# A two-layer transformer kernel on one core: three pairs of PSUM banks in turn for the first attention, and one bank for the row maxima of the second

## What is computed

```python
xn = _layernorm(x)
x  = x + attn0(xn) + ffn0(xn)          # layer 0
xn = _layernorm(x)
x  = x + attn1(xn) + ffn1(xn)          # layer 1

def attn0(x):      # 16 heads of 64 channels, causal; "dense" below
    k, q, v = W_K x, W_Q x, W_V x
    scores = tril(k . q) ; attn = softmax(scores / sqrt(64))
    z = v . attn ; return W_O z

def ffn0(x):       # conv, 16 heads of 8 channels with rotary angles, causal softmax,
    ...            # projection, then a routed layer of 4 experts; "early", "ahead", "after"
def attn1(x):      # block-wise softmax, 16 heads of 8 channels; "behind"
def ffn1(x):       # 4-bit rounding of inputs and weights, gate, up, down; "behind"
```

## Time and profile before

| | us |
|---|---|
| median of 3 executions | 3603.09 (3598.25 to 3603.40) |
| the profiled execution's own time | 3598.52 |
| its span, first to last instruction | 3596.7 |
| PE busy | 3086.5 (86%) |
| DVE, ACT, POOL busy | 2093.3, 1787.1, 860.3 |
| mean granted TensorE clock, of full speed | 0.937 |

### The profile page before, as it was taken

The page is one execution under the profiler, slowest core; times in us unless marked ns, Lnnn a source line. Parts: engine busy times, 40 slices in busy tenths (PEclk is TensorE's granted clock), DMA queues, the critical chain, the costliest instruction groups (busy, mean ns, idle before and its releaser), DMA issues.

```text
span 3596.7 us, 53224 instructions
## 1 busy us (share of the span) xinstructions
PE 3086.5 (86%) x19535; PEld 1705.8 (47%) x19535; DVE 2093.3 (58%) x4810; ACT 1787.1 (50%) x4252; POOL 860.3 (24%) x1140
## 2 busy tenths in 40 slices
PE   2689898998989899998989889898988989898864
PEld 1245455454545545454545545454554545454432
DVE  5454665756566575657656565665656566554432
ACT  0245555555545455555545555554555555455421
POOL 0000222313222131323123132312213131222323
PEclk7699999999999999999999999999999999999965
DMA  4130303020020302002030301103020110200000
GB/s 104 20 44 1 52 2 47 9 36 20 13 43 2 55 2 44 12 17 40 1 55 2 44 12 22 35 2 55 2 44 12 24 31 7 47 2 14 6 11 3
DMA packets 112901, 89.39 MB, mean 25 GB/s; under 512 B 11203, under 2 KB 107269, under 8 KB 112645
## 3 DMA queue, kind: packets, MB, share of 16 engines
q1 hardware_dynamic: 93956, 70.25, 12.8%
q0 software_dynamic: 4096, 8.40, 0.8%
q10 hardware_dynamic: 14592, 7.34, 0.7%
HBM read 27.05 MB, written 16.19 MB: 12 GB/s over the span
## 4 chain that ended last, share of the span: by engine, by line
PE 59%; DVE 12%; POOL 10%; issue 9%; ACT 5%; DMA 2%; SPq 1%; POOLq 0%; ACTq 0%; DVEq 0%
PE ps L1584 6%; PE ps L1601 6%; PE ps L1819 4%; PE ps L1743 4%; PE ps L1722 4%; PE ps L1656 3%; PE ps L1645 3%; PE ps L1623 3%; DVE nma L1210 3%; PE ps L1632 3%; PE ps L1574 2%; PE ps L1703 2%; PE ps L1884 2%; PE ps L1561 2%; PE ps L1587 2%
## 5 line engine op out<-in xcount | busy, mean ns | idle before, releaser
L877 ACT ACTIVATE share_a<-ps,nma 128x128 f32<-128x128 f32 (+3 forms) x1024 | 530.9, 525 | 443.7 <-DVE nma L1210 442.5
L1210 DVE TENSOR_REDUCE nma<-ps 128x2 f32<-128x256 f32 (+3 forms) x512 | 420.1, 823 | 407.5 <-PE ps L1587 405.4
L945 ACT ACTIVATE share_z<-ps 128x512 f32<-128x512 f32 (+1 forms) x704 | 378.3, 559 | 372.1 <-PE ps L1724 241.7
L1275 DVE TENSOR_REDUCE nmx<-ps 128x1 f32<-128x384 f32 (+3 forms) x704 | 426.1, 635 | 173.9 <-PE ps L1705 162.4
L722 POOL TENSOR_TENSOR vn<-va,rla 128x512 f32<-128x512 f32 x128 | 133.4, 1042 | 1359.1 <-DVE rla L1181 1359.1
L1601 PE MATMUL ps<-share_a,vn 128*64 128x512 f32 (+3 forms) x2048 | 351.4, 492 | 35.7 <-POOL vn L722 34.7
L1703 PE MATMUL ps<-kst,qst 96*128 96x128 bf16 (+3 forms) x1024 | 269.6, 317 | 71.1 <-DMA kst<-part 34.4
L1722 PE MATMUL ps<-qst,kst 99*128 99x512 bf16 (+3 forms) x1024 | 261.6, 304 | 28.2 <-ACT share_z L945 14.9
L798 POOL TENSOR_TENSOR share_s<-share_s 128x352 f32<-128x352 f32 (+1 forms) x80 | 80.1, 1001 | 770.7 <-DVE share_s L1084 770.5
L1601 PEld LDWEIGHTS ps<-share_a,vn 128*64 128x64 f32 x2048 | 150.8, 151 | 227.9 <-issue 154.2
L1584 PE MATMUL ps<-kq_odd 64*128 64x128 f32 (+3 forms) x1024 | 220.5, 508 | 38.7 <-ACT share_a L877 36.9
(11 more groups left out here) (250 smaller groups left out, 5727.0 us busy)
## 6 DMA issues: line engine op xcount, KB each, us to landing
qst<-part SPq DMA_DIRECT2D x144, 128.0 KB
kst<-part SPq DMA_DIRECT2D x144, 128.0 KB
share_r<-h_sorted SPq DMA_DIRECT2D x16, 448.0 KB, 3.5
y_sorted<-share_a ACTq DMA_DIRECT2D x16, 448.0 KB, 3.0
xin<-in_L_attn_x SPq DMA_DIRECT2D x16, 256.0 KB, 3.9
xk<-xn SPq DMA_DIRECT2D x16, 256.0 KB, 17.5
xres<-in_L_attn_x SPq DMA_DIRECT2D x16, 256.0 KB
out<-xn SPq DMA_DIRECT2D x16, 256.0 KB, 17.4
```

The source lines that it names most:

```text
L877: activation(pa[:, h % 4, OFF[t]:OFF[t] + P * (t + 1)], ps[:, b + k, 0:P * (t + 1)], ACT.Exp, bias=nma[:, h, t:t + 1], accum_out=la[:, h, ...
L945: activation(pt[:, n % 2, h % 4:h % 4 + k, 0:wd], src, ACT.Exp, scale=SCALE_B)\
L1210: v.tensor_reduce(nma[:, 2 * p:2 * p + 2, t], ps[:, b:b + 2, 0:P * (t + 1)], AX.X, ALU.max, negate=True).then_inc(amax, 1)
L1275: v.tensor_reduce(nmx[:, h:h + k, t], src, AX.X, ALU.max, negate=True).then_inc(bmax_ready, 1)
```

## The change

`RING` becomes a ring of three places (banks 0 and 1, 2 and 3, 4 and 5). The values of pair p+2 share a place with `z(p)`, each in one bank of it, so `v` and `z` are in the ring. `row_max` and the small steps before it all use bank 6, and `row_max(u)` waits for the maxima of unit u-1. `exps` still alternates between banks 5 and 6 and now waits once for the last copy of `z`.

```diff
-RING = [("kq", 0), ("kq", 1)]
+SLOTS = 3
+RING = [("kq", 0), ("vv",), ("kq", 1)]
 for _p in range(PAIRS):
-    RING += [("scores", _p, _t) for _t in range(NT)] + ([("kq", _p + 2)] if _p + 2 < PAIRS else [])
+    RING += [("scores", _p, _t) for _t in range(NT - 1)] + ([("zv", _p - 1)] if _p else [])
+    RING += [("scores", _p, NT - 1)] + ([("kq", _p + 2)] if _p + 2 < PAIRS else [])
+RING.append(("zv", PAIRS - 1))
+def ring_bank(*unit):
+    return 2 * (RING_AT[unit] % SLOTS)
+def v_bank(p):
+    return ring_bank("vv") + p if p < 2 else ring_bank("zv", p - 2) + 1
...
                 def ring_turn(*unit):
                     n = RING_AT[unit]
-                    if n >= 2:
-                        kind, p, *t = RING[n - 2]
+                    if n >= SLOTS:
+                        kind, *at = RING[n - SLOTS]
                         if kind == "kq":
-                            pe.wait_ge(kq_ready, count(i, DENSE["kq_ready"], p + 1))
+                            pe.wait_ge(kq_ready, count(i, DENSE["kq_ready"], at[0] + 1))
+                        elif kind == "vv":
+                            pe.wait_ge(av_ready, count(i, DENSE["av_ready"], 2))
+                        elif kind == "zv":
+                            pe.wait_ge(z_ready, count(i, DENSE["z_ready"], at[0] + 1))
+                            pe.wait_ge(av_ready, count(i, DENSE["av_ready"], min(at[0] + 3, PAIRS)))
                         else:
-                            pe.wait_ge(aexp_done, count(i, DENSE["aexp_done"], 8 * p + 2 * t[0] + 2))
+                            pe.wait_ge(aexp_done, count(i, DENSE["aexp_done"], 8 * at[0] + 2 * at[1] + 2))
...
                 def row_max(u):
                     t, h0, k = MAX_UNITS[u]
-                    wd, b = P * (t + 1), 5 + u % 2
+                    wd, b = P * (t + 1), 6
                     if u == 0:
                         pe.wait_ge(bv_ready, count(nxt, AHEAD["bv_ready"], 1))
                         pe.wait_ge(stack_loaded, count(nxt, EARLY["stack_loaded"], 16 * 18))
-                    if u >= 2:
-                        pe.wait_ge(bmax_ready, count(nxt, AHEAD["bmax_ready"], u - 1))
+                    else:
+                        pe.wait_ge(bmax_ready, count(nxt, AHEAD["bmax_ready"], u))
...
                 def divide(t):
-                    if t >= 2:
-                        pe.wait_ge(yn_ready, count(i, AHEAD["yn_ready"], t - 1))
+                    else:
+                        pe.wait_ge(yn_ready, count(i, AHEAD["yn_ready"], t))
 ORDERS pe, one line of many:
-        2), ("scores1", 0), ("row_max", 3), ("row_max", 4), ("scores1", 1), ("row_max", 5), ("row_max", 6),
+        ("row_max", 3), ("values1",), ("row_max", 4), ("scores1", 0), ("row_max", 5), ("scores1", 1),
```

More of the change, by code:

```diff
@@ L141, with z_bank @@
+def z_bank(p):
+    return ring_bank("zv", p)
+def v_bank(p):
+    return ring_bank("vv") + p if p < 2 else ring_bank("zv", p - 2) + 1
 ORDERS = dict(
     pe=[
[L143 to L146, removed]
@@ L162 @@
[L162 to L166, removed]
@@ L177 @@
[L177 to L180, removed]
+        ("divide", 0), ("kq", 0), ("v", 0), ("divide", 1), ("kq", 1), ("scores", 0, 0), ("divide", 2), ("v",
+        1), ("divide", 3), ("scores", 0, 1), ("join",), ("scores", 0, 2), ("project_y",), ("scores", 0, 3),
@@ new lines @@
+        ("kq", 2), ("scores", 1, 0), ("scores", 1, 1), ("scores", 1, 2), ("z", 0), ("v", 2), ("scores", 1, 3),
+        ("transpose3",), ("route",), ("kq", 3), ("scores", 2, 0), ("scores", 2, 1), ("scores", 2, 2),
+        ("rank",), ("z", 1), ("v", 3), ("project_v",), ("scores", 2, 3), ("kq", 4), ("row_max", 0),
[3 rows of a table added]
+        ("row_max", 9), ("scores1", 5), ("scores", 3, 1), ("row_max", 10), ("scores1", 6), ("row_max", 11),
+        ("scores1", 7), ("row_max", 12), ("scores", 3, 2), ("row_max", 13), ("z", 2), ("row_max", 14), ("v",
@@ new lines @@
+        36), ("scores", 6, 3), ("probs_T1", 1, 1), ("scores", 7, 0), ("row_max", 37), ("scores", 7, 1),
+        ("row_max", 38), ("probs_T1", 1, 2), ("row_max", 39), ("scores", 7, 2), ("probs_T1", 1, 3),
+        ("row_max", 40), ("z", 6), ("scores", 7, 3), ("row_max", 41), ("mix1", 1), ("row_max", 42),
+        ("row_max", 43), ("z", 7), ("project1",), ("shift_rows",), ("sort",), ("ao",), ("exps", 0), ("exps",
+        1), ("gate", 0), ("value", 0), ("exps", 2), ("exps", 3), ("transpose1",), ("gate", 1), ("value", 1),
@@ L191 @@
[L191 to L195, removed]
@@ L201 @@
-        43), ("mix1", 1), ("norm", 7), ("project1",), ("shift_rows",), ("round_x", 0), ("round_x", 1),
-        ("round_x", 2), ("ln0_stats",), ("ln0_root",), ("ln0_apply",), ("ln1_apply",), ("add_ao",), ("gate",
+        ("ln2_root",), ("scores", 2, 2), ("place",), ("scores", 2, 3), ("ln2_apply",), ("row_max", 0),
+        ("row_max", 1), ("row_max", 2), ("row_max", 3), ("values1",), ("row_max", 4), ("row_max", 5),
+        ("row_max", 6), ("scores", 3, 0), ("row_max", 7), ("row_max", 8), ("block_max1", 0), ("row_max", 9),
@@ L203 @@
+        39), ("row_max", 40), ("scores", 7, 2), ("scores", 7, 3), ("row_max", 41), ("norm", 7), ("row_max",
+        42), ("row_max", 43), ("mix1", 1), ("project1",), ("round_x", 0), ("round_x", 1), ("shift_rows",),
+        ("ln0_stats",), ("ln0_root",), ("ln0_apply",), ("ln1_apply",), ("round_x", 2), ("add_ao",), ("gate",
         0), ("value", 0), ("gate", 1), ("value", 1), ("gate", 2), ("value", 2), ("conv",), ("project", 0, 0),
-        ("up1", 0), ("project", 0, 1), ("split", 0), ("round_h", 0, 0), ("gate", 3), ("round_h", 0, 1),
@@ new lines @@
+        ("scores", 7, 1), ("scores", 7, 2), ("z", 6), ("scores", 7, 3), ("z", 7), ("sort",), ("exps", 0),
+        ("exps", 1), ("gate", 0), ("exps", 2), ("exps", 3), ("transpose1",), ("gate", 1), ("exps", 4),
+        ("turn", 0), ("exps", 5), ("exps", 6), ("transpose_xq",), ("down", 0), ("gate", 2), ("exps", 7),
+        ("exps", 8), ("exps", 9), ("turn", 1), ("exps", 10), ("gate1", 0), ("exps", 11), ("attend", 0, 3),
+        ("down", 1), ("exps", 12), ("gate", 3), ("exps", 13), ("gate1", 1), ("exps", 14), ("turn", 2),
```

172 lines of the change are left out of this document (80 added, 92 removed), and 23 rows, old and new, of tables (act, pe, pool).

## The result

The changed kernel takes 3736.65 us (median of 4 executions, 3735.5 to 3738.62) against 3602.35 us before: 1.0376 times, 95% interval 1.0358 to 1.0394. It is slower, as forecast, but by 134 us and not by 14, and outside the range.

A forecast was written before the change was run, and what follows sets the result against it. PE, busy for 86% of the span, was taken to set the pace. Short turn +30, full turns -11, last dense turn -5 gave +14 us, added to the median of 3603.1: 3617 us, range 3573 to 3660.

The forecast's parts named there:

- part 4: Rest of a full turn, behind `z(3)`: moved steps covered, +0.3 us for single handovers; whole turn -0.7 us, 15 turns -11 us.
- part 1: Short turn: 44 row maxima alone on one bank no longer overlap PE with DVE, +30 us (bounds +24 to +32).
- Part 2: Full turns: ring and `v`/`z` bank cost 5.8 us a turn, partly regained; waits for exponentials fall from 74 below 35 us.
- Part 3: Full turns up to `z(3)`: waits at `row_max(0)`, layer-1 scores, units 16 to 20 and POOL take back part 2's gain.
- Part 5: Last dense turn, without `row_max`: half of the waits for ring and `v` come home, -5 us (bounds 0 and -12).
- The clock rival: Waits at `row_max(0)` and units 17 to 20 lower PE's clock, +2 us a turn, 3660 us; chance 0.20.

The follow-up runs named there:

- e5: Kernel before with one line added, `sort` waiting for the copy of z(7) before its first matmul: 3688.53 us against 3606.79, 1.0232 times.
- e1: Changed kernel with PE's seven loads of expert numbers moved from `sort` into `ao`, wait of `sort` kept: 3631.13 us, 1.0077 times before.
- e2: Changed kernel with the short turn's 44 row maxima on banks 5 and 6 in turn as before: 3702.63 us, 1.0276 times before.
- e7: Changed kernel with e1's and e2's edits, two ring places left unused and no wait in `sort`: 3586.53 us, 0.995 times before.
- e6: Kernel before with the seven loads of expert numbers moved from `sort` into `ao`: 3579.71 us, 0.9929 times before.
- e4: Kernel before with `row_max` on bank 6 alone and two of DVE's row maxima one place earlier: 4163.41 us, 1.1559 times before.
- e10: Kernel before with e4's two moves of DVE's row maxima, but two banks for `row_max` as before: 3630.66 us, 1.0071 times before.
- e9: Changed kernel with the seven loads of expert numbers in `sort` done twice, fourteen in all: 3804.48 us, 1.0546 times before.

## Why the prediction was wrong

**The step that failed** is in part 4: "The moved `shift_rows` has `sort` and `ao` (8 us of PE) as cover". The passage prices the end of the turn by what PE computes there, and has no term for the wait that the change adds to `sort`, nor for what is queued behind it. It asked what stands behind `z(7)` on the engine, but not what the sequencer does between the matmuls. The missing term is 82 us by e5 (5.1 us in each of 16 turns), and 105 us are got back by taking the loads away from the place (e1). The trace of before could have shown it: the loads of L1615 take 4.4 us there, of which 0.32 us stand bare, and their cover was what the new wait took away. The forecast that the change is slower was not luck: without the missed term the other two measured ones, +34 and +7 us, would still have made it slower, as forecast by part 1.

**Part 1, +30 us: right.** 64.29 us against 33.38 is +30.9 us in the stretch, e2 gives 30.2 us at the first `sort` and 34 us in the whole. A unit of 512 columns takes the 1.50 us worked out.

**Part 2, the ring: right in its mechanism.** PE's waits for the ring went from 74.4 us to 33 us (19.1, 8.3 and a third line of 5.6 for the copy of `va`), under the 35 named; `v` no longer waits.

**Part 3, what takes it back: right in kind, and in its sum by luck.** Forecast and measured in the turn from 2041.15: `row_max(0)` 1.6 and 1.50 us, `route` (from part 2) 0.9 and 0.87, the six gaps between the layer-1 scores 0.45 each and 0.20 to 0.45, together 2.3 us and not 2.7. The units 16 to 20 waited for 0.16 + 1.03 + 1.19 + 0.90 = 3.3 us and not 5.3. Two waits were missed, and their 2.4 us fill up what was too much elsewhere, 10.4 us in all where 10.5 us were forecast: `project_v`, which was moved ahead, 1.13 us for DVE's `expert_i`, and `scores(3, 2)` 1.25 us for the copy of `kq(4)`. The rows of PE:

```profile
2147.99 1.05 PE L1792 MATMUL ps<-wrt,share_h 128*128 128x4 f32 x8 [0.87 <-ACT share_h L979]
...
2159.03 1.13 PE L1706 MATMUL ps<-wbv,hc 128*128 128x128 f32 x8 [1.13 <-DVE expert_i L1374]
2164.72 0.23 PE L1720 MATMUL ps<-kst,qst 96*128 96x128 bf16 x1 [1.50 <-ACT vones L948]
...
2187.14 0.92 PE L1605 MATMUL ps<-kq_odd 64*128 64x384 f32 x4 [1.25 <-ACT share_g L873]
2188.55 2.37 PE L1617 MATMUL ps<-share_a,vn 128*64 128x512 f32 x16
```

The sum, -0.7 us a turn, came out as +0.7 us in e7 against e6, within the bounds of -4.4 to +4.8; with the spread of e6's turns the sign is not shown. `z(3)`, which I had as the end of the chain, does not wait for POOL in this turn (no idle time at 2207.92), nor in the turn of e7 from 1952.6 on: PE comes to it late, 160.5 us behind `sort` in e7, where before it was 159.6 us, the last 1.60 us of them waiting.

**Part 5, the last dense turn, -5 us:** e7 against e6 gives -9.0 us, within the bounds; the changed kernel itself has 208.9 against 202.2 us, for this stretch, from one `sort` to the next, begins with the same loss in front of `ao` and in it.

**The sum again, with the measured terms:** +34 (short turn, e2), +82 (`sort`'s wait, e5), +7 (banks and order with the loads mended, e7 against e6): 123 of 134 us. The 11 us left may be the parts working on each other; no run splits them.

**The clock rival** named the right price, a lower clock behind a wait, but not the place that cost most: `ao` is 30 us slower in all. At the units 17 to 20 the clock did fall as the rival said:

```profile
2198.00:2208.20 10.20, 9.30 (x37) 3.98 (x37) 7.01 (x15) 5.59 (x17) 4.73 (x19) 0.50 0.00 0
```

In return the two slow `z` of the turn before (at 1852.76 and 1948.46, 4.07 us each) take 2.37 us after (at 2154.44 and 2038.00). With the loads mended the inner turns are 207.95 us (e1), as long as before (208.0), so this fall of the clock did not make the loss.

The rule beside that rival, that small idle times of PE between groups of matmuls, from cycling through banks, make the clock swing, is from the Trainium skill, TensorE: Matmul & The Clock Gate, section "A second HAM failure mode: psum-queue depth-cycling". The traces agree with it in the old order with one bank: the mean granted clock of e4 is 0.885, of its control e10 0.935. In the new order it does not decide: e7 has 0.941, before 0.937.

With the one term of part 4 the forecast would have been 3617 + 82 = 3699 us, still 38 us low.

## What to carry over

When a change adds a wait on an engine, list what its sequencer does behind the wait that is not a matmul. Here the place of seven register loads cost 27 us in 16 turns while matmuls already queued covered most of them; one new wait in front uncovered them, and the clock of what followed was lower too: 82 us more. Look whether the last user of a ring of banks shares a bank with the next step, for that is what made the wait necessary; two unused places in the ring removed it here, in a run that came out 11 us better than the sum of its parts. The price of sharing one bank depended on what DVE had to do between two reads: some 0.7 us a unit where it only reads, 1.4 us for a wait in the old order, much less with the units spaced. A price from one stretch does not hold for another.

## What the runs showed of the hardware

- A load of a register from memory by PE's sequencer took 0.63 us from start to start (0.30 us the load, 0.15 us the work on the registers behind it, the rest between them); with their number doubled, each of the 112 additional ones cost 0.61 us of the run's time (e9).
- Behind 3.68 us of standing still (after) and 3.57 us (e5), 64 matmuls of `ao` took 9.99 and 9.34 us at a mean granted clock of 0.72 and 0.75; without the gap they took 7.31 us (e1), at 1.00.
- A slower PE can nearly pay for itself: in the kernel before, `z(7)` at a granted clock of 0.57 took 1.7 us longer (4.07 against 2.37 us), and PE stood still behind `sort` for 0.32 us where behind a fast `z(7)` it was 1.75 us. Of these 1.75 us only some 0.8 us are the loads': with them moved away (e6) PE still waits 1.0 us there for a DMA.
- The same instructions in the same order took 203.5 to 209.3 us from turn to turn in one run (e6), with more stretches at 1.2 GHz in the long turns.
